# Loading the first two heads' key and query stacks from GpSimd's queue inside the projection stage, and starting head 1's row maxima with head 0's first tile

## The reference

```python
qkv = x @ W_qkv.T                       # x is layer-normalised, 2048 x 512
q, k, v = jnp.split(qkv, 3, axis=-1)    # then 16 heads of 32
attn = jnp.einsum('bhqd,bhkd->bhqk', q, k) * SCALE
attn = jnp.where(causal, attn, -jnp.inf)
probs = jax.nn.softmax(attn, axis=-1)
out = jnp.einsum('bhqk,bhkd->bhqd', probs, v)
out = out @ W_proj.T
x = x + layernorm(out)                  # then x + layernorm(moe(layernorm(x)))
```

## Time and profile before

| | us |
|---|---|
| median of the runs | 1784.22 (1782.85 to 1786.0) |
| the profiled execution's own time | 1782.18 |
| its span in the profile | 1780.4 |
| TensorE busy in the span | 1651.6 (93%) |
| mean granted TensorE clock | 0.969 |

### The profile page before, as it was taken

The page is one execution under the profiler, slowest core; times in us unless marked ns, Lnnn a source line. Parts: engine busy times, 40 slices in busy tenths (PEclk is TensorE's granted clock), DMA queues, the critical chain, the costliest instruction groups (busy, mean ns, idle before and its releaser), DMA issues.

```text
span 1780.4 us, 30680 instructions
## 1 busy us (share of the span) xinstructions
PE 1651.6 (93%) x9215; PEld 1370.4 (77%) x9215; DVE 1168.5 (66%) x2386; ACT 1100.2 (62%) x1668; POOL 949.6 (53%) x828
## 2 busy tenths in 40 slices
PE   6999899999999999998785999999999999999990
PEld 6977577667777677775564899999999999999980
DVE  5526677777777777777478566666666565566534
ACT  2211687778877887876477466666666565556542
POOL 2310588878888888886653343433433434334324
PEclk9999899999999999999996899999999999999995
DMA  7565311222111111110571887987987787788768
GB/s 237 165 185 158 84 49 49 68 63 60 47 47 47 47 47 47 48 48 30 190 285 53 264 255 206 280 249 214 275 248 219 226 256 218 213 241 232 219 156 195
DMA packets 103221, 276.87 MB, mean 156 GB/s; under 512 B 19851, under 2 KB 37643, under 8 KB 93131
## 3 DMA queue, kind: packets, MB, share of 16 engines
q1 hardware_dynamic: 76059, 212.25, 36.8%
q0 software_dynamic: 27056, 63.31, 16.9%
HBM read 194.76 MB, written 63.72 MB: 145 GB/s over the span
## 4 chain that ended last, share of the span: by engine, by line
PE 39%; DMA 4%; POOL 3%; DVE 3%; issue 3%; ACT 1%; POOLq 0%; DVEq 0%; ACTq 0%
PE p_prj L85 22%; PE p_at_ps L85 6%; PE p_logit_ps L85 6%; PE p_ht_ps L1940 3%; DMA acc_rows<-m_y_out,m_row_ids 2%; PE p_at_ps L1963 2%; DMA m_gate<-acc_rows 1%; POOL rows L1332 1%; POOL p_rstd L1318 1%; DVE r_lane_hot L1645 1%; ACT r_edge_hot L1421 1%; DVE p_st L1657 1%; DVE p_st L1651 1%; POOL p_minus L1316 0%; POOL gathered L1347 0%
## 5 line engine op out<-in xcount | busy, mean ns | idle before, releaser
L683 POOL TENSOR_TENSOR prob_lo<-prob,prob_hi 128x1024 fp32r<-128x1024 f32 x217 | 465.5, 2164 | 103.8 <-DVE prob_hi L763 97.2
L735 DVE TENSOR_REDUCE part_max<-a_mp 128x1 f32<-128x512 f32 (+2 forms) x600 | 359.9, 610 | 72.6 <-PE a_mp L818 39.0
L1354 POOL DMA_INDIRECT acc_rows<-m_y_out,m_row_ids x109 | 177.6, 1629 | 418.6 <-ACT m_y_out L1525 389.5
L719 ACT ACTIVATE prob<-a_sp 128x1024 f32<-128x1024 f32 x320 | 293.7, 930 | 70.0 <-PE a_sp L881 39.2
L85 PE MATMUL p_prj<-m_w_hi,m_ht_hi 128*128 128x352 f32 x888 | 297.7, 335 | 1.5 <-DVE m_ht_lo L1754 1.5
L85 PE MATMUL p_prj<-m_w_lo,m_ht_hi 128*128 128x352 f32 x888 | 288.8, 325 | 0.0
L85 PE MATMUL p_prj<-m_w_hi,m_ht_lo 128*128 128x352 f32 x888 | 288.3, 325 | 0.0
L1778 DVE TENSOR_TENSOR m_w_lo<-m_w_raw,m_w_hi 128x704 fp32r<-128x704 f32 (+1 forms) x357 | 271.1, 798 | 22.9 <-ACT m_w_hi L1531 22.4
L1531 ACT ACTIVATE m_w_hi<-m_w_raw 128x704 fp32r<-128x704 f32 (+1 forms) x357 | 229.0, 713 | 16.8 <-PE p_prj L85 16.8
L1764 DVE TENSOR_TENSOR m_at_lo<-p_at_ps,m_at_hi 128x384 fp32r<-128x384 f32 x111 | 61.8, 557 | 252.8 <-ACT m_at_hi L1517 252.8
L706 ACT ACTIVATE prob_hi<-prob 128x1024 fp32r<-128x1024 f32 x216 | 203.3, 941 | 6.9
(11 more groups left out here) (242 smaller groups left out, 3351.9 us busy)
## 6 DMA issues: line engine op xcount, KB each, us to landing
m_w_raw<-wexp SPq DMA_DIRECT2D x51, 1408.0 KB, 6.9
m_w_raw<-wexp SPq DMA_DIRECT2D x51, 768.0 KB, 6.3
qk_parts<-rows SPq DMA_DIRECT2D x64, 256.0 KB, 3.1
multi<-qk_parts SPq DMA_DIRECT2D x48, 256.0 KB, 4.6
acc_rows<-p_zeros SPq DMA_DIRECT2D x2, 4352.0 KB, 17.4
v_head<-v_all SPq DMA_DIRECT2D x16, 520.0 KB, 3.1
k_stack<-qk_parts SPq DMA_DIRECT2D x24, 256.0 KB, 3.9
q_stack<-qk_parts SPq DMA_DIRECT2D x24, 256.0 KB, 6.0
```

Source lines behind the costliest of these rows:

```text
L683: nc.gpsimd.tensor_tensor(prob_lo[:, t % RING, :, c0:NB], prob[:, t % RING, :, c0:NB], f32(prob_hi[:, t % RING, :, c0:NB]), ALU.subtract). ...
L719: nc.scalar.activation(prob[:, t % RING, :, c0:NB], sp_[:, t % 2, :, c0:NB], ACT.Exp, scale=SCALE).then_inc(prob_ready, 1)
L735: nc.vector.reduce_max(part_max[:, qb, kb:kb + 1], mp[:, n % 2, 0:width], AX_X).then_inc(piece_done, 1)
L1354: nc.gpsimd.indirect_dma_start(acc_dram[sum_of(t)], bass.IndirectOffsetOnAxis(ap=row_id(t), axis=0), y_out[:, t % 4, :], None, compute_op= ...
```

## The change

- The six loads of head 0's stacks move from SyncE's queue to GpSimd's. GpSimd waits for the eight units' transfers and issues three loads after piece 0, three after piece 1.
- The second pair of stacks is allocated ahead of both stages (`stack1`). The projection stage keeps two of its three weight slots in it. When unit 23 is computed, GpSimd writes the ones row of `k_stack` and issues the six loads of head 1 there.
- The attention stage's own `load_head(1, 1)`, its ones row and the wait of TensorE for it go away. SyncE's wait for all transfers stands behind the loads of v.
- The units are written out for all engines instead of running partly in loops with registers. `parked` is four pairs' worth of semaphores (one pair per piece) instead of one pair.
- Head 0 takes head 1's pieces by a table of its own, `PIECES_AT_FIRST`, with two in each of steps 0 to 4 and mostly two after that.

```diff
-            def first_head(n):
-                for at, stack, parts in ((PIECE_UNITS, 0, (2, 3, 2)), (2 * PIECE_UNITS, 1, (0, 0, 1))):
-                    if n == at:
-                        for k in range(2):
-                            sp.wait_ge(parked[k], 16 * n)
-                        for i, part in enumerate(parts):
-                            sp.dma_start(f32(multi[i * HD:(i + 1) * HD, stack, :]), qk_dram[part, 0:HD, :]
-                                         ).then_inc(head0_landed, 16)
-            qk_units(sp, park, first_head)
+            qk_units(park)
...
+            def load_stack(h, dst, parts):
+                for i, part in enumerate(parts):
+                    nc.gpsimd.dma_start(f32(dst[i * HD:(i + 1) * HD, :]), qk_dram[part, h * HD:(h + 1) * HD, :]
+                                        ).then_inc(early_landed[h], 16)
+            for q, parts in ((0, (2, 3, 2)), (1, (0, 0, 1))):
+                for k in range(2):
+                    pool.wait_ge(*parked_unit((q + 1) * PIECE_UNITS - 2 + k))
+                load_stack(0, multi[:, q, :], parts)
+            pool.wait_ge(unit_ready, 3 * PIECE_UNITS)
+            pool.wait_ge(head0_ones, 1)
+            nc.gpsimd.memset(f32(stack1[0][ROW_MAX:ROW_MAX + 1, :]), 1.0).then_inc(head0_ones, 1)
+            for stack, parts in zip(stack1, ((2, 3, 2), (0, 0, 1))):
+                load_stack(1, stack, parts)
...
-        w_hi = sb("e_w_hi", [P, 3, KC, PIECE], F32R)
-        w_lo = sb("e_w_lo", [P, 3, KC, PIECE], F32R)
+        w_hi, w_lo = ([stack[:, i * T // 2:(i + 1) * T // 2].rearrange("p (c n) -> p c n", c=KC) for i in range(2)] + [last[:]]
+                      for stack, last in zip(stack1, (sb("e_w_hi2", [P, KC, PIECE], F32R), sb("e_w_lo2", [P, KC, PIECE], F32R))))
...
 PIECES_AT = (0, 0, 0, 0, 0, 3, 4, 3, 4, 2, 1, 2, 1, 3, 3, 3, 3, 3, 3, 2)
+PIECES_AT_FIRST = (2, 2, 2, 2, 2, 3, 3, 2, 2, 2, 1, 2, 1, 2, 2, 2, 2, 2, 2, 2)
...
+            sp.wait_ge(head0_max_landed, 32)
             load_v(0, 0)
-            for k in range(2):
-                sp.wait_ge(parked[k], 16 * QK_PIECES * PIECE_UNITS)
-            sp.wait_ge(head0_max_landed, 32)
             def head(h, p, visit, first, last):
                 if not last:
                     if not first:
                         sp.wait_ge(scores_ready, h * NS)
-                    load_head(h + 1, 1 - p)
-                    if not first:
+                        load_head(h + 1, 1 - p)
                         sp.wait_ge(pv_done, h * NS)
                     load_v(h + 1, 1 - p)
+                    if first:
+                        for pair in parked:
+                            for one_parity in pair:
+                                sp.wait_ge(one_parity, 32 * PIECE_UNITS // 2)
```

More of the change, by code:

```diff
@@ L513, with pieces_at, first_part_done @@
 PIECES_AT = (0, 0, 0, 0, 0, 3, 4, 3, 4, 2, 1, 2, 1, 3, 3, 3, 3, 3, 3, 2)
-PIECES_AT_A = next(t for t in range(NS) if sum(PIECES_AT[:t]) >= NPC_A)
-assert sum(PIECES_AT) == NPC and NS == len(PIECES_AT) and NS % RING == 0
+PIECES_AT_FIRST = (2, 2, 2, 2, 2, 3, 3, 2, 2, 2, 1, 2, 1, 2, 2, 2, 2, 2, 2, 2)
+assert sum(PIECES_AT) == sum(PIECES_AT_FIRST) == NPC and NS == len(PIECES_AT) == len(PIECES_AT_FIRST) and NS % RING == 0
+def pieces_at(t, first, last):
+    table = PIECES_AT_FIRST if first else PIECES_AT
+    return [] if last else list(range(sum(table[:t]), sum(table[:t + 1])))
+def first_part_done(first):
+    table = PIECES_AT_FIRST if first else PIECES_AT
+    return next(t for t in range(NS) if sum(table[:t]) >= NPC_A)
 SHARED_AT = {3: "max_b", 6: 3, 9: 0, 15: 1, 16: "max_a", 18: 2}
@@ L776, in head @@
                         row_maxima(h, "b")
-                    if t == PIECES_AT_A and not last:
+                    if t == first_part_done(first) and not last:
                         row_maxima(h + 1, "a")
-                    pieces = [] if last else list(range(sum(PIECES_AT[:t]), sum(PIECES_AT[:t + 1])))
+                    pieces = pieces_at(t, first, last)
                     for n in pieces[:1]:
@@ L888, in head @@
                         pe.wait_ge(max_b_landed[p], (visit + p) * 16)
-                    pieces = [] if last else list(range(sum(PIECES_AT[:t]), sum(PIECES_AT[:t + 1])))
+                    pieces = pieces_at(t, first, last)
                     if t == LAG:
                         pe.wait_ge(v_landed[p], visit * 16 + 16)
-                    if first and t == NS - 1:
-                        pe.wait_ge(ones_set, 1)
                     if t == 0:
```

97 lines of the change are left out of this document (44 added, 53 removed).

## The result

The changed kernel took 1774.56 us in the median of six runs (1773.13 to 1779.71) and the kernel before 1785.22 us beside it on the same chip (1782.85 to 1790.45). The ratio is 0.9946, with a 95% interval of 0.9934 to 0.9957: faster by 0.54%, 9.7 us of 1784.2 (the two medians side by side give 10.7 us). The forecast was 12.1 us and 1772.0 us.

The account below looks back on a forecast made before the run. TensorE, busy 93%, was taken as the bound, so only its waits and low clock could give time. 5.6 + 1.8 - 0.3 + 0 + 5.0 = 12.1 us off 1784.2 gave 1772.1 us, range 1766 to 1778.5.

Parts of the forecast that it names:

- First gap: TensorE's 3.23 us wait after SyncE held unit 8, plus 2.9 us of low clock; 0.5 us stays, gain 5.6 us.
- a backlog of 2.7 us against a slack of 1.8: In the first gap: loads delay a transfer by at most 2.7 us, units absorb 1.8, leaving 0.9 us at worst.
- Second gap: TensorE's 3.02 us wait around unit 16's loads; 1.2 us stays, with the first piece waiting for loads; gain 1.8 us.
- Head 1's loads: 1.5 MB loaded in units 24 and on, beside the units' transfers; loss 0.3 us, from 0 to 0.9.
- the slack of 4.5 us: In units 24 and on: delay the transfers can absorb, as a unit with pieces lasts about 3.6 us; backlog 5.4 us.
- Written-out units, ones row, SyncE's waits: In the units and head 0: these edits cost or gain zero, from -0.5 to +0.8 us.
- Head 0: First head of attention: from 44.97 to 40.0 us as load waits and low clock shrink; gain 5.0 us, between 1 and 8.
- the floor of 36.3: Head 0's 44.97 us without 4.2 us of waits and 4.5 us lost at low clock; costs were added to it.
- The rule weighed: Loads moved to GpSimd's queue: by the rule little more than SyncE's 1.6 us would come back in each gap.
- Traffic did not set the gaps alone: Rival for both gaps: shared DMA engines keep them as long, with the low clock; 4.7 us gained, 1779.5 us; chance 0.12.
- Head 0 did get shorter: Rival said the opposite: ScalarE and GpSimd chains keep head 0 long; gain 8.1 us, 1776.1 us; chance 0.14.
- The loads were late by 1.6 us at most: Rival: loads on GpSimd's queue take 18.6 us, stalling TensorE 13.8 us in unit 20; 1787.6 us; chance 0.05.

Follow-up runs that it names:

- e2_pad: The changed kernel with 32 bytes left free ahead of the second pair of stacks and 32 ahead of `xT`; ratio 0.9924, 1775.57 us.
- e11_best_from20: As e10_best, with head 0's pieces starting one unit later, over ten units instead of eleven; ratio 0.9922 to the kernel before, 1773.89 us.
- e12_after: The changed kernel unaltered, for a third profile and more runs; ratio 0.9949 to the kernel before, 1775.76 us.
- e6_phase: The changed kernel with four small LayerNorm tiles allocated behind the weights, so weights and `xT` lie a multiple of 1024 bytes apart; ratio 0.9946, 1775.91 us.
- e10_best: The changed kernel with e2_pad's first pad, e6_phase and e4_paced in one; ratio 0.9927 to the kernel before, 1774.17 us.
- e4_paced: The changed kernel with head 1's six loads issued one per unit, not in one group; ratio 0.9921 to the kernel before, 1774.97 us.
- e1_after: The changed kernel unaltered, for a second profile; ratio 0.9930 to the kernel before, 1776.72 us.
- e3_old_table: The changed kernel with the old table of pieces for head 0, none in steps 0 to 4; ratio 0.9929 to the kernel before, 1776.31 us.
- e7_sp: The changed kernel with head 0's six loads back on SyncE's queue, with its waits ahead of units 8 and 16; ratio 0.9990, 1781.81 us.
- e8_all: The changed kernel with e4_paced and e6_phase, head 0's loads paced too, pieces one unit later, large tensors at multiples of 64 bytes; ratio 0.9933, 1771.77 us.

## Why the prediction was right, and where its terms were not

The median, the range and the sign were right: 1774.56 against 1772.0, in 1766 to 1778.5. The sum was 2.4 us too high, and terms in it erred by more than that.

**First gap, forecast 5.6 us of gain.** The wait in unit 14 was 2.04, 1.2 and 1.13 us in three executions, not 0.5. In one of the three it brought 3.4 us at clock 0.50 with it, which costs 1.7 us. I had priced a backlog of 2.7 us against a slack of 1.8, and taken about half of the 0.9 left. In 107 to 115 the DMA engines move 217 GB/s at a share of 0.83, so 261 at full share where I had 290 from the earlier trace rows: the backlog is 2.9 us and 1.1 are left, which is what two of the executions show. So the bound of 0.9 was already too low, by the bandwidth in it, and the choice of 0.5 below it added to that. The 2.0 us of the first profile are more than this working gives, as are 1.8 in e2_pad and 2.2 in e11_best_from20, and why these executions differ is open. Each of the three has 3.4 us of low clock behind the gap: that a gap shorter than 3.0 us leaves the clock up did not hold. Gain: 6.1 - 2.0 - 1.7 = 2.4 us in the profile of after, 6.1 - 1.1 = 5.0 in e12_after.

**Second gap, forecast 1.8 us.** 3.02 became 1.38 and 1.29 us, a gain of 1.6 to 1.7. The size was right and the mechanism was not: the loads of `multi`, which landed within 5.2 us where I had taken 6.1, were there for the first piece, and what TensorE waited for was VectorE's maximum behind a late low part, the contention that the term only mentions. That the number agrees is luck. The loads were late only in other placements and paces of the matmuls (0.7 us in e6_phase, 1.6 in e10_best).

**Head 1's loads, forecast -0.3 us, range to 0.9.** This is the term that was mis-sized. It cost 2.1 us in two executions and 3.8 in a third, with 3.4 us of low clock in it. The backlog was as priced at worst: the slowest transfer landed 8.5 us after issue instead of 3.1, which is 5.4 us. The step that failed is the slack of 4.5 us, and with it the 0.3 taken below its bound; 5.4 less the 2.1 measured leaves 3.3. The slack was counted up to the start of unit n+2, but with pieces TensorE needs VectorE sooner, as in unit 20: a piece within unit n+1 waits for a maximum that stands behind the low part of unit n. The wait at 166.39 is one. e4_paced removes it.

**Placement, not in the sum at all.** 1.1 us in the units and some 0.6 us in the products with v, from the addresses of weights and `xT`. The diff shows that the weights move; I had read it as a change of names. e6_phase undoes the first part.

**Written-out units, ones row, SyncE's waits: nothing.** Nothing shows. SyncE's issues run through from 95.11 on.

**Head 0, forecast 5.0 us.** 4.8 to 5.4, less 0.3 to 0.5 that head 1 lost, which was not forecast. The total was right and its parts were not. The low clock, which was to cost 1.7 us instead of 4.5, lasted 11.3 us of head 0 in after and 9.1 and 9.2 in e1_after and e12_after, and costs 4.5 to 5.7 us: none of it came back. GpSimd and ScalarE, for which I added 2.0, cost at most 0.4: after 198.6 TensorE is busy for 28.35 of 28.40 us, and the one wait in head 0 of e1_after is 0.4. And the head less these is 34.5 to 34.7 us, not the floor of 36.3. That errors of about 3 us each way met is luck. e3_old_table, treated in the same way (42.97 less 1.4 of waits and 6.1 of low clock), comes to 35.5; so the old table, beyond the waits that it caused, is 0.8 to 1.0 us of the difference, and the rest is open.

**The rule weighed.** e7_sp against after is the test of who issues. The second issuer moved the wait for the landed units out of SyncE's way, and gave 2.7 us of stretch and ratios apart by 0.4%. The Trainium skill ("DMA: Bandwidth & Descriptors", "Issuing engines are not separate DMA queues") would have it save the sequencer's time alone. Its other half, that all issuers share the same DMA engines, this trace bears out: the loads from GpSimd delay SyncE's transfers, with ScalarE's waits of 2.81 to 5.16 us beside them.

**The rivals.** Traffic did not set the gaps alone, but kept 2.4 to 5.1 of the 9.1 us at stake in the two gaps (6.1 and 3.0), and more in head 1's loads. Head 0 did get shorter. The loads were late by 1.6 us at most, in e10_best, and not at all in after.

**The share that the clock has.** Against the first profile of before the three profiled executions gained 2.3, 2.4 and 7.7 us of span, and at like clock it is some 7; the median has 10 because the changed kernel's runs have a clock higher by 0.003 in the mean. I took terms of one execution off a median. That the result came within 2.6 us of the forecast owes something to this: terms forecast at 12.1 us are worth about 7 at like clock, and some 3 us of clock came on top. How much of that is the change's own doing is open. The sum counted on 2.9 us of clock behind the first gap and 2.8 in head 0; in the units the three profiled executions lost 1.7, 1.7 and 0 us by it where both of before lost 3.4, and in head 0 nothing came back.

## What to carry to other kernels

Take a wait and the loads behind it out of the queue that other transfers need, and then spread the loads: six at once cost more than the same six at one for each step of the work. A table that puts work earlier needs its loads earlier too: alone it lost, where the early loads alone did not. Before a wait is put down to a load, look which of the matmuls on that line it is, and when the loads landed. Where the diff moves a buffer that feeds TensorE, look at the distance from one matmul's start to the next, and compare executions at the same mean clock before a few microseconds are explained.

## What the hardware showed that was not expected

- The pace of a 512-column matmul in fp32r depends on where its two operands lie: 227 ns with weights and `xT` a multiple of 1024 bytes apart (before, e6_phase, e8_all, e10_best) and 233.4 to 234.3 ns otherwise (e2_pad, after). Only five placements were tried, and the two slow ones are 192 and 160 bytes off, so a multiple of 128, 256 or 512 bytes would fit as well: that this is the rule is not shown.
- The kernel before has a mean granted clock between 0.964 and 0.971 from run to run, and the means of the table above go from 1788.1 to 1783.4 us with it. A thousandth of clock is worth 0.9 us here, as much as some of the edits.
- Loads of 256 KB on GpSimd's queue took 0.49 us each to issue (0.79 the first). Head 0's six landed in 3.9 to 6.6 us in after, and in 3.1 to 4.6 on SyncE's queue in e7_sp; head 1's six, all at once on GpSimd's queue, took 5.0 to 8.3, and 3.8 to 4.6 spread over six units in e4_paced.
